# Masked attention on one core: the projection kept as one fp32 copy, values by fp32 transposes

## What is computed

```
# x: (16, 512, 1024), mask: (16, 1024) of 0 and 1, Wq and Wo: 512 x 512, 8 heads of 64
xt = transpose(x, (0, 2, 1))
q = xt @ Wq.T
qh = q.reshape(B, T, 8, 64).transpose(0, 2, 1, 3)      # queries, keys and values are the same
scores = einsum('bhqd,bhkd->bhqk', qh, qh) / 8
logits = (scores * cmask + (1 - cmask) * -1e30) * rmask
attn = softmax(logits, axis=-1)
ctx = einsum('bhqk,bhkd->bhqd', attn, qh)
out = (ctx back to (B, T, D)) @ Wo.T
x + transpose(out, (0, 2, 1))
```

## Time and profile before

| | |
|---|---|
| median of 3 runs | 1617.94 us (1615.75 to 1622.37) |
| profiled execution, own time | 1618.75 us |
| its span, first to last instruction | 1617.0 us |
| mean granted TensorE clock | 0.979 |
| TensorE busy | 1537.4 us, 95% |
| GpSimd busy | 1339.3 us, 83% |
| VectorE busy | 1187.3 us, 73% |
| ScalarE busy | 850.0 us, 53% |

### The profile page before, as it was taken

How to read it: one execution, slowest core, us unless ns; L and a number is a source line. 1 busy time by engine, 2 the same in 40 slices (tenths; PEclk the granted TensorE clock), 3 DMA queues, 4 the chain that set the end, 5 groups by cost and what they waited for, 6 DMA issues and landing times. The chain is left out here.

```text
span 1617.0 us, 33177 instructions
## 1 busy us (share of the span) xinstructions
PE 1537.4 (95%) x10956; PEld 1222.1 (76%) x10956; DVE 1187.3 (73%) x2659; ACT 850.0 (53%) x2055; POOL 1339.3 (83%) x1069
## 2 busy tenths in 40 slices
PE   6798999999999999999999999999999999999995
PEld 3666778787877778787777778777877777777863
DVE  5356787877878787777878778787877778787773
ACT  2145655565555556555555555555555555555450
POOL 5558989889898989889898988989898897987771
PEclk9689999999999999999999999999999999999997
DMA  3433454444445445354444535444544544453410
GB/s 115 104 83 94 111 129 119 113 122 106 122 106 127 122 110 130 98 130 102 123 122 111 136 93 131 101 121 122 123 127 99 129 106 117 115 131 90 108 50 30
DMA packets 93810, 179.09 MB, mean 111 GB/s; under 512 B 24704, under 2 KB 24832, under 8 KB 93632
## 3 DMA queue, kind: packets, MB, share of 16 engines
q1 hardware_dynamic: 64448, 109.71, 29.2%
q0 software_dynamic: 29184, 67.17, 14.5%
HBM read 36.77 MB, written 33.55 MB: 43 GB/s over the span
## 5 line engine op out<-in xcount | busy, mean ns | idle before, releaser
L870 DVE TENSOR_REDUCE small_mxp<-max_scores 108x1 f32<-108x270 f32 x1280 | 547.9, 436 | 269.0 <-PE max_scores L1069 209.3
L751 ACT ACTIVATE small_Pt<-scores,small_kbias 108x270 f32<-108x270 f32 x1280 | 553.0, 484 | 351.7 <-PE scores L1088 335.6
L596 POOL TENSOR_TENSOR small_Pacc<-small_Pacc,small_Pt 108x540 f32<-108x540 f32 x384 | 517.7, 1348 | 116.4 <-ACT small_Pt L751 109.7
L1069 PE MATMUL max_scores<-small_ops 128*108 128x270 f32 x1280 | 412.8, 329 | 17.8 <-DVE small_mxp L870 16.7
L1100 PE MATMUL ctx_psum<-small_Pt,small_V 108*64 108x270 f32 x2560 | 314.7, 393 | 0.0
L900 DVE RECIPROCAL small_rsum<-small_rsum 128x67 f32<-128x67 f32 (+1 forms) x512 | 240.7, 532 | 74.9 <-ACT small_rsum L698 59.5
L1069 PEld LDWEIGHTS max_scores<-small_ops 128*108 128x108 f32 x1280 | 219.1, 173 | 87.6 <-issue 43.4
L1085 PE MATMUL scores<-small_ops 128*108 128x270 f32 x1280 | 270.4, 290 | 4.7 <-ACT small_Pt L751 4.0
L1100 PEld LDWEIGHTS ctx_psum<-small_Pt,small_V 108*64 108x64 f32 x2560 | 185.1, 137 | 107.3 <-issue 0.5
L1088 PE MATMUL scores<-small_ops 128*108 128x270 f32 x1280 | 263.6, 287 | 0.0
L1085 PEld LDWEIGHTS scores<-small_ops 128*108 128x108 f32 x1280 | 191.8, 173 | 25.3 <-issue 9.4
(11 more groups left out here) (108 smaller groups left out, 2356.6 us busy)
## 6 DMA issues: line engine op xcount, KB each, us to landing
small_ops<-small_H SPq DMA_DIRECT2D x512, 135.0 KB
small_ops<-small_L SPq DMA_DIRECT2D x256, 135.0 KB
small_ops<-small_mrow SPq DMA_DIRECT2D x128, 2.1 KB
small_xg<-x_rows,small_idx POOLq DMA_INDIRECT x80, 4.1
small_xtail<-x_rows,small_idx POOLq DMA_INDIRECT x80, 3.7
out_rows<-small_xtail,small_idx POOLq DMA_INDIRECT x80, 3.1
out_rows<-small_xg,small_idx POOLq DMA_INDIRECT x80, 3.3
wq_sb<-wq SPq DMA_DIRECT2D x1, 1024.0 KB, 5.5
```

Source lines behind the costliest of these rows:

```text
L596: nc.gpsimd.tensor_tensor(acc, other, t["Pt"][:R, p0], ALU.add).then_inc(pacc_step, 1)
L751: nc.scalar.activation(t["Pt"][:R, (NT * s + k) % f.NP, half, :], ST[(2 * (NT * h + k) + half) % 3][:R, 0:H], ACT.Exp, bias=t["kbias"][:R, ...
L870: nc.vector.tensor_reduce(t["mxp"][:R, h % 2, m // 2, m % 2:m % 2 + 1], MX[m % 2][:R, 0:H], AX.X, ALU.max).then_inc(mx_red, 1)
L1069: nc.tensor.matmul(MX[m % 2][:R, 0:H], ops[:, OPA, tile_cols(m // 2)], ops[:, OPB, half_cols(m % 2)], start=True, stop=True).then_inc(mx_r ...
```

## The change

q of a half is first copied from the bank to a new fp32 tile `q` (two stages, as `H`), with a semaphore `q_kept`. ScalarE then makes `H` from that copy, and waits for its own first copy before. VectorE makes `L` from `q` and `H`, both in SBUF. TensorE may refill the bank after `q_kept`. A value job waits for `q_kept` of both halves and makes one fp32 transpose of `q` for each tile, in place of the two products. All this holds for the form "small" alone (`copies_q`). In the "small" form this makes 128 more copies on ScalarE, and 320 transposes in place of 640 matmuls.

```
+        self.copies_q = split and self.C <= 540
...
+            if f.copies_q:
+                keep("q", [P, 2, f.C], F32)
...
-                        nc.scalar.copy(t["H"][:, g % 2, cols], MB[bank][:, 0:H]).then_inc(hi_done, 1)
+                        if f.copies_q:
+                            nc.scalar.copy(t["q"][:, g % 2, cols], MB[bank][:, 0:H]).then_inc(q_kept, 1)
+                            act.wait_ge(q_kept, 2 * p + half + 1)
+                            nc.scalar.copy(t["H"][:, g % 2, cols], t["q"][:, g % 2, cols]).then_inc(hi_done, 1)
+                        else:
+                            nc.scalar.copy(t["H"][:, g % 2, cols], MB[bank][:, 0:H]).then_inc(hi_done, 1)
...
-                        nc.vector.tensor_tensor(t["L"][:, g % 2, cols], MB[bank][:, 0:H],
+                        nc.vector.tensor_tensor(t["L"][:, g % 2, cols], t["q"][:, g % 2, cols] if f.copies_q else MB[bank][:, 0:H],
                                                 t["H"][:, g % 2, cols].bitcast(F32), ALU.subtract).then_inc(lo_done, 1)
...
-                        at_least(pe, lo_done, 2 * (PAIRS * b + arg[0]) + arg[1] + 1)
+                        at_least(pe, q_kept if f.copies_q else lo_done, 2 * (PAIRS * b + arg[0]) + arg[1] + 1)
...
-                        pe.wait_ge(lo_done, 2 * (PAIRS * b + g) + 2)
+                        pe.wait_ge(q_kept if f.copies_q else lo_done, 2 * (PAIRS * b + g) + 2)
                         for i in range(min(4, NT - 4 * part)):
                             cols = tile_cols(4 * part + i)
+                            if f.copies_q:
+                                last = nc.tensor.transpose(mb[:R, P * i:P * i + P], t["q"][:, g % 2, cols],
+                                                           identR[:].bitcast(F32))
+                                continue
```

More of the change, by code:

```diff
@@ L334, in attention_kernel @@
         exp_done, xT_kept, hi_done, v_kept = sem("exp_done"), sem("xT_kept"), sem("hi_done"), sem("v_kept")
+        q_kept = sem("q_kept")
         xbar_kept, w_kept, ct_kept = sem("xbar_kept"), sem("w_kept"), sem("ct_kept")
```

## The result

The changed kernel takes 1686.51 us (median of 4 runs, 1683.13 to 1690.13) against 1617.40 for the kernel before in the same series. The ratio is 1.0428, with a 95% interval of 1.041 to 1.0447. The forecast was 1624 with a range of 1601 to 1638: the kernel is 69 us slower, where 5 to 6 were forecast, and 48.5 us above the upper end. The profiled execution has a span of 1686.4 us, against 1617.0.

A forecast was written before the change was run, and what follows sets the result against it. TensorE was taken as the bound, busy 92.19 of 93.6 us a batch. Net 0.31 us a batch saved, times 15, gives 4.7 us; one lost race adds 10: 1618.75 - 4.7 + 10 = 1624 us, range 1601 to 1638.

The forecast's parts named there:

- the price of the subtraction's wait: VectorE's L885, now with two SBUF inputs, waits for the rest of one GpSimd addition, up to 1.3 us, 128 times.
- the other six halves: Subtractions outside (0,4) and (4,4), above all (5,4): waits mostly end in VectorE idle time, 0.19 us a batch allowed.
- the clock 1 in 100: Rival: transposes not counting as work lower TensorE's clock, 2.2 us 64 times, giving 1760 us; chance 1 in 100.
- The race at (4,4): Subtraction asks at 433.92, GpSimd's L584 starts about 433.86: lost by 0.06, TensorE about 0.8 later, +0.67 us a batch.
- The race at (0,4): Subtraction asks about 383.91, before GpSimd's L596 at 383.97, so waits only for L561; if lost, +0.67 us a batch.
- the forecast's case of one lost: One of the races at (0,4) and (4,4) lost, 10 us: 1624 us, range 1619 to 1629, chance 0.36.
- Transposes on TensorE: Five transposes replace ten matmuls per pair: 0.45 us goes, 0.36 at the four-tile part and 0.09 at the last tile.
- nothing is kept at (4,0): At (4,0) TensorE follows a VectorE reduce with 0.05 us spare, so only 0.05 of the pair's 0.45 is kept.
- The second copy: ScalarE: 0.42 us plus 0.04 wait per half; TensorE waits 0.23 at (1,0), and (5,0)'s pair comes to -0.13.
- The slow one: Rival: both races, at (0,4) and (4,4), lost, giving 1634 us; chance 0.16 for 1630 to 1638.
- All that was dearer than 1634: Transposes, clock or GpSimd dearer than reckoned: above 1634 us, chance 0.07.
- with (4,0) free: Rival where VectorE and ScalarE give way: 1600 us, 1590 if (4,0) loses nothing too; chance 0.24 for 1590 to 1609.

The follow-up runs named there:

- experiment 1: Changed kernel, but VectorE's subtraction reads q from the PSUM bank again and the bank is held until it is done: 1621.84 us, ratio 1.0013.
- Experiments 5: Kernel before, with values made by one fp32 transpose of H, low part left out, no q or second copy: 1607.65 us, ratio 0.9941.
- experiment 3: Changed kernel, with a one-column GpSimd memset behind each of the 80 additions of w to the tail: 1687.45 us, ratio 1.042.
- second kernel of experiment 7: Changed kernel, with GpSimd waiting ahead of its addition in (0,1) until the subtraction is done: 1635.62 us, ratio 1.0092.
- experiment 8: experiment 1 with ScalarE's copies to ctxT moved to (1,0) and (5,2), subtractions behind them later, L915 in (5,3): 1718.26 us, ratio 1.0596.
- experiment 4: Changed kernel, with the tail additions of (0,0), (0,1) moved to later places, five now from (0,3) to (1,3): 1663.88 us, ratio 1.0276.
- the run in which the stretches were shorter by one addition: Changed kernel, with GpSimd waiting ahead of its addition in (0,2) until the subtraction is done: 1652.07 us, ratio 1.0205.

## Why the prediction was wrong, by its own steps

**The step that failed: the price of the subtraction's wait.** The prediction said that the subtraction waits for the rest of one addition, up to 1.3 us, and that "most of these waits end in idle time". For the half finished in (0,1) it measured 5.09 us, over the rest of one addition and three more behind it. The term of the sum that stood for it was the 0.19 a batch for "the other six halves"; it cost 2.9 at (0,3) and (0,4). The run of additions was in the trace of the kernel before, behind L561 which starts there at 375.69, and was not looked at, because only (0,4) and (4,4) were taken for races:

```profile
376.92 1.32 POOL L596 TENSOR_TENSOR small_Pacc<-small_Pt 108x540 f32<-108x540 f32 x1
378.21 1.26 POOL L561 TENSOR_TENSOR small_xtail<-small_xtail,small_w 108x512 f32<-108x512 f32 x1
379.44 1.34 POOL L596 TENSOR_TENSOR small_Pacc<-small_Pacc,small_Pt 108x540 f32<-108x540 f32 x1
```

I generalised from another instruction, L905. Its longest sample got in at a gap of 0.18 us: the addition ends at 550.71, and GpSimd's next instruction, a gather, starts at 550.89. But having looked at runs would not have settled it. In the kernel before, L905 at (1,1) asks with further additions queued behind the running one, and gets in at the first hand-over in 15 of 15 batches, at 0.81 to 0.83 us each:

```profile
477.57 1.36 POOL L596 TENSOR_TENSOR small_Pacc<-small_Pacc,small_Pt 108x540 f32<-108x540 f32 x1
478.70 0.81 DVE L905 TENSOR_TENSOR small_ctxT_lo<-small_ctx,small_ctxT 128x540 fp32r<-128x540 f32 x1
478.89 3.00 POOL L561 TENSOR_TENSOR small_xtail<-small_xtail,small_w 108x512 f32<-108x512 f32 x2
```

So no sample in the trace of before showed VectorE being passed over, and 5.09 was at most to be had as an upper bound. The mechanism (an exclusion between VectorE with two SBUF inputs and GpSimd) was right, as experiment 1 shows; its size was not. I had cited the Trainium skill, SBUF — State Buffer, "Who interferes with whom", for the exclusion. That section also says that the order of issue decides who blocks. The trace does not agree with that here: the subtraction had asked 0.92 us before L601 started, and was overtaken three times.

**The step that was missing: idle time has a price of its own.** I gave the clock 1 in 100, for transposes. Experiments 5 and 1 ran at 1.00 with all transposes, so that reason falls as I thought. But the clock fell at the two idle stretches of (0,3), and 21 of the 69 us are due to it. The Trainium skill, TensorE: Matmul & The Clock Gate, "HAM oscillation — how this bites in real kernels", tells of waits for DMA between bursts of matmuls that bring the clock down. The trace agrees that waits of TensorE do it, though here they were for VectorE and, at 0.73 and 1.34 us, shorter than those of that section. It would have changed the price of any long wait.

**The race at (4,4): right in place and size.** The forecast had it lost by 0.06 us, with TensorE 0.8 us later than before. It was lost, in all fifteen batches, by 0.005 to 0.018 between the start of L589 and that of the subtraction in the kernel after:

```profile
646.23 1.27 POOL L589 TENSOR_TENSOR small_xsum<-small_xsum,small_xtail 108x512 f32<-108x512 f32 x1
646.24 1.56 DVE L895 TENSOR_TENSOR small_L<-small_q,small_H 128x270 fp32r<-128x270 f32 x1 [0.29 <-ACT small_H L691]
```

The windows give -0.35 at (5,0) and +1.16 at (5,1): 0.81 together. Taking away the exclusion alone (experiment 1) leaves +0.51 of the 1.16, so the exclusion costs 0.65 there, for a forecast of 0.67. That so thin a margin fell the forecast way is luck; the price is not. Experiment 3 shows how thin it is: in three of its fifteen batches with this place the subtraction asks 0.002 to 0.003 us ahead of that addition instead of 0.009 to 0.024 behind it, and takes 0.44 instead of 1.56. In the two of them that are among the fourteen, (5,1) loses 0.51, as without the exclusion, but (6,1) then loses 2.73.

**The race at (0,4): won, as in the forecast's case of one lost.** With the long wait gone (second kernel of experiment 7) the subtraction there takes 0.56 us, and (1,1) loses 0.37, as with no exclusion at all (0.36). In the changed kernel itself the long wait moves what comes behind it, and the subtraction there takes 1.31 (median).

**Transposes on TensorE: nearly right at four tiles, wrong at the last.** The four-tile part gives 0.31 to 0.34 in place of 0.36, with one record for each transpose (320). The fifth tile gives nothing, not 0.09: (0,3) takes 1.82 us in the second kernel of experiment 7, and took 1.79. The timeline of the kernel after shows what comes last there:

```profile
588.45 0.19 PEld L1143 LDWEIGHTS misc<-small_xcT,small_wqT_hi 128*128 128x128 f32 x1 [0.20 <-ACT small_V L700]
```

The projection behind the last tile needs the bank that ScalarE is still copying to `V`. A stretch that ends at a bank in use gives nothing back. That nothing is kept at (4,0) was right, to 0.05.

**The second copy: right in duration, near in price.** It measured 0.418, where I took 0.42, and its wait about 0.04. The loss at (1,1) was 0.36 where I had 0.23, so too low; at (5,1) it was 0.51 where the working gives 0.58. With all that, the gain without any exclusion is 0 a batch (experiment 1) and not 0.50. So even the half of the working that stood was too favourable by 8 us.

**What the rivals said.** None had this case. The slow one, both races lost at 1634, had the right mechanism at the wrong place, priced with one addition. What decided was neither race but the half finished in (0,1), and the run of additions there. All that was dearer than 1634 had a chance of 0.07. One sum of the rivals does not come out either: with (4,0) free, 0.40 more a batch would give 1594 and not 1590.

## What to carry to other kernels

Before an instruction of VectorE gets a second SBUF input, list for each of its places how many GpSimd instructions stand back to back from that moment on. The upper bound of its wait is the whole run, not the rest of one; at (1,1) of the kernel before L905 got in at the first hand-over each time, in (0,2) of the changed kernel L895 at none. Where VectorE is followed closely by TensorE, a source in PSUM is worth keeping, even if a bank is held longer: here no loss could be put down to holding it (experiment 1), and reading the copy in SBUF cost 4%. And price idle stretches of TensorE of one or two microseconds with the low clock that may follow: here 1.6 us each time.

## What was not expected of the hardware

- A VectorE subtraction with two SBUF inputs was overtaken three times by queued GpSimd additions (5.09 us instead of 0.43), and 5.67 us instead of 0.71 in experiment 8. In the rows above it got in at gaps of 0.19, 0.27 and 0.59 us.
- Without a gap either engine can win. VectorE won behind L601 at 590.29 in experiment 4, and at (1,1) of the kernel before in 15 of 15 batches; it lost behind L566 at 585.29 in the kernel after. At each of these two places it goes the same way in every batch. What decides this stays open; none of the runs tells it apart.
- A GpSimd memset of one column between two additions overlaps both and opens no gap (experiment 3).
- The granted clock fell to 0.50 for about 3.5 us at two idle stretches of 0.73 and 1.34 us with few matmuls between them, in 13 of 14 batches of the changed kernel and in 8 of 14 of experiment 3, whose stretches are as long. It stayed at 1.00 in all batches of the run in which the stretches were shorter by one addition.
